# A two-layer attention and gated-MLP kernel on one core: two more score products inside the first layer, score tiles 4 to 7 in other PSUM banks, and the general-weight code moved behind the last batch

## The reference, cut to what matters

```python
xn = layernorm(x)
# attention of the first layer, one head of width 128
k, q, v = xn @ Wk.T, xn @ Wq.T, xn @ Wv.T
ak = k @ Wa.T
alpha = softmax(q @ ak.T)          # 1024 x 1024 scores for each batch
s = alpha @ (v @ Wb.T)
# MLP of the first layer, ternary weights with a scale for each output
h = silu(lin(xn, w1)) * lin(xn, w2)   # the gated units, 512 wide
h = gelu(lin(h, h1)); h = gelu(lin(h, h2))
g = lin(h, w3)
```

## Time and profile before

| | |
|---|---|
| median of three runs | 1051.15 us |
| profiled execution, device time | 1052.17 us |
| its span (first to last instruction) | 1050.3 us |
| TensorE busy | 980.8 us, 93% of the span |
| ScalarE busy | 759.2 us, 72% |
| VectorE busy | 560.3 us, 53% |
| GpSimd busy | 197.7 us, 19% |
| mean granted TensorE clock | 0.988 of full speed |
| one batch, start to start | about 254 us |

### The profile page before, as it was taken

One profiled execution on the slowest core, in us unless ns is written; L12 is line 12 of the kernel. 1 busy time (PEld: TensorE's weight loads), 2 busy tenths in 40 slices (PEclk: granted clock), 3 DMA queues, 4 the chain that ended last, 5 costly groups with the idle time before them and its releaser, 6 DMA issues.

```text
span 1050.3 us, 16258 instructions
## 1 busy us (share of the span) xinstructions
PE 980.8 (93%) x6122; PEld 548.5 (52%) x6122; DVE 560.3 (53%) x1372; ACT 759.2 (72%) x926; POOL 197.7 (19%) x144
## 2 busy tenths in 40 slices
PE   3999899999999989999989989999999998999995
PEld 2788633343478843334358874334436886333431
DVE  6655734635546653554564574455446457346252
ACT  5444699989753479998955358998885436999885
POOL 1100202512300020341130002043122002025023
PEclk9999899999999999999999999999999999999998
DMA  6000032000000013100000002300000000310000
GB/s 239 1 2 1 13 49 50 1 2 1 5 19 2 1 30 49 34 1 2 1 21 2 1 1 46 65 3 1 1 1 21 2 1 13 50 30 1 1 1 23
DMA packets 14428, 20.66 MB, mean 20 GB/s; under 512 B 2848, under 2 KB 11136, under 8 KB 14080
## 3 DMA queue, kind: packets, MB, share of 16 engines
q1 hardware_dynamic: 14336, 19.41, 8.6%
HBM read 7.85 MB, written 2.10 MB: 9 GB/s over the span
## 4 chain that ended last, share of the span: by engine, by line
PE 76%; DVE 8%; ACT 7%; issue 6%; POOL 2%; DMA 0%; DVEq 0%; POOLq 0%; ACTq 0%
PE ps L1097 73%; ACT big L1053 4%; PE ps L1501 1%; DVE st L277 1%; DVE wk L543 1%; POOL st L867 1%; DVE xn L449 1%; DVE wk L733 1%; ACT xn L1025 1%; ACT qz L1001 1%; DVE wk L474 1%; DVE flags L417 1%; PE ps L1117 1%; DVE qk_max L558 0%; PE ps L1494 0%
## 5 line engine op out<-in xcount | busy, mean ns | idle before, releaser
L1053 ACT ACTIVATE big<-ps 128x1024 f32<-128x1024 f32 x512 | 493.8, 1034 | 50.8 <-PE ps L1097 48.7
L1097 PE MATMUL ps<-big,vaug 128*32 128x512 f32 x2048 | 272.6, 604 | 3.8 <-DVE wk L733 2.6
L1097 PE MATMUL ps<-hid 32*128 32x512 f32 x1024 | 130.6, 493 | 3.7 <-ACT big L1053 2.5
L1097 PE MATMUL ps<-hid,fw_sb 128*128 128x512 f32 x416 | 100.7, 396 | 0.0
L969 ACT ACTIVATE wk<-ps,cols_sb 128x512 f32<-128x512 f32 x64 | 40.5, 687 | 78.3 <-PE ps L1097 74.3
L867 POOL TENSOR_TENSOR st<-st 128x4 f32<-128x4 f32 x16 | 16.2, 1011 | 423.3 <-DVE st L532 315.2
L1097 PEld LDWEIGHTS ps<-hid 32*128 32x128 f32 x1024 | 49.1, 181 | 77.2 <-issue 41.6
L1097 PEld LDWEIGHTS ps<-hid,fw_sb 128*128 128x128 f32 x416 | 77.7, 188 | 17.8
L880 POOL TENSOR_TENSOR qz<-qz,wk 128x512 f32<-128x512 f32 x32 | 41.1, 1286 | 232.8 <-DVE wk L703 232.8
L1097 PEld LDWEIGHTS ps<-big,vaug 128*32 128x32 f32 x2048 | 41.0, 108 | 69.8 <-issue 42.2
L721 DVE SCALAR_TENSOR_TENSOR big<-ps,sm,big 128x128 f32<-128x128 f32 x128 | 44.2, 345 | 46.9 <-PE ps L1097 35.9
(11 more groups left out here) (210 smaller groups left out, 1618.5 us busy)
## 6 DMA issues: line engine op xcount, KB each, us to landing
hid<-spl SPq DMA_DIRECT2D x288, 32.0 KB
xnext<-in_x SPq DMA_DIRECT2D x4, 512.0 KB, 3.9
out<-qz SPq DMA_DIRECT2D x8, 256.0 KB, 2.3
big<-in_fw SPq DMA_DIRECT2D x1, 1877.0 KB, 8.9
wk<-in_lw SPq DMA_DIRECT2D x1, 1476.0 KB, 13.9
big<-in_fw SPq DMA_DIRECT2D x1, 939.0 KB, 10.7
cst_sb<-in_cst SPq DMA_DIRECT2D x1, 440.0 KB, 4.4
xn<-in_aw SPq DMA_DIRECT2D x1, 320.0 KB, 5.0
```

The source lines that it names most:

```text
L1053: up(ms_exp, a.activation(prob[:, at:at + 2 * CH].rearrange("p (h n) -> p h n", n=CH), ps[:, bank:bank + 2, :], ACT.Exp, scale=HDM ** -0.5))
L1097: return t_.matmul(out_, lhsT, rhs, start=start, stop=stop, **kw)
```

## The change

Four edits, all in TensorE's program but for one bank table that ScalarE's exponentials read too.

- `SC_BANKS` becomes a table of 16: tiles 0 to 3 and 8 to 15 stay in banks 2, 3, 6, 7, tiles 4 to 7 go to banks 0, 1, 4, 5, those of the gated units 2 and 3. Tile 4 then waits for the gate of unit 2, tile 6 for that of unit 3 (`gated`), tiles 8 to 11 for the exponentials of tiles 0 to 3, tiles 12 to 15 for those of tiles 8 to 11.
- The products of tile 3 are made ahead of `l1_unit(0, 2)`, those of tile 2 behind it, after a wait for `neg_ok` (bank 6 holds the transposed maxima until then). The loop then adds only the maxima to the first four tiles.
- Both `t_.If` are replaced by branches whose exact target stands right behind them.
- The general code of all batches stands once each behind the last batch, and jumps back.

```diff
-MAX_BANKS, SC_BANKS = (2, 6), (2, 3, 6, 7)
+MAX_BANKS, SC_BANKS = (2, 6), (2, 3, 6, 7, 0, 1, 4, 5, 2, 3, 6, 7, 2, 3, 6, 7)
@@ scalar
-                                            ps[:, SC_BANKS[n_ % 4], :], ACT.Exp))
+                                            ps[:, SC_BANKS[n_], :], ACT.Exp))
@@ tensor
                 def score_products(n_):
                     h, jt = n_ // NT, n_ % NT
                     sl = slice(h * CH, (h + 1) * CH)
-                    split3(ps[:, SC_BANKS[n_ % 4], :], *tok(jt), spl[:, 0, sl], spl[:, 1, sl], True, False)
+                    split3(ps[:, SC_BANKS[n_], :], *tok(jt), spl[:, 0, sl], spl[:, 1, sl], True, False)
...
                     t_.transpose(ps[0:NT, 6, 0:P], mx[:, :], ident).then_inc(maxT.sem, 1)
+                    score_products(3)
                     l1_unit(0, 2, general)
+                    t_.wait_ge(neg_ok.sem, neg_ok.at(b, 1))
+                    score_products(2)
                     l1_unit(0, 3, general)

-                with t_.If(wide > 0):
-                    first_layer(True)
-                with t_.Else():
+                t_.br_lt(wide, 1, on_true="t_exact1_%d" % b, on_false="t_general1_%d" % b)
+                with nc.body("t_exact1_%d" % b, valid_engines=[t_.engine]):
                     first_layer(False)
-
-                t_.wait_ge(neg_ok.sem, neg_ok.at(b, 1))
+                    t_.br("t_scores_%d" % b)
+                attended.close()
+                attended.enter_context(nc.body("t_scores_%d" % b, valid_engines=[t_.engine]))
+
                 t_.wait_ge(negrow_in.sem, negrow_in.at(b, 16))
                 for n_ in range(2 * NT):
+                    if n_ in (4, 6):
+                        t_.wait_ge(gated.sem, gated.at(b, n_ // 2 + 1))
+                    elif 8 <= n_ < 12:
+                        t_.wait_ge(sc_exp.sem, sc_exp.at(b, n_ - 7))
+                    elif n_ >= 12:
+                        t_.wait_ge(sc_exp.sem, sc_exp.at(b, n_ - 3))
                     if n_ >= 4:
-                        t_.wait_ge(sc_exp.sem, sc_exp.at(b, n_ - 3))
-                    if n_ >= 2:
                         score_products(n_)
                     h = n_ // NT
-                    up(sc_mm, mm(ps[:, SC_BANKS[n_ % 4], :], one_row[:, :], shift[:, h * CH:(h + 1) * CH], False, True))
+                    up(sc_mm, mm(ps[:, SC_BANKS[n_], :], one_row[:, :], shift[:, h * CH:(h + 1) * CH], False, True))
...
-                with t_.If(wide > 0):
-                    mlp_rest(True)
-                with t_.Else():
+                t_.br_lt(wide, 1, on_true="t_exact2_%d" % b, on_false="t_general2_%d" % b)
+                with nc.body("t_exact2_%d" % b, valid_engines=[t_.engine]):
                     mlp_rest(False)
+                    t_.br("t_second_%d" % b)
+                attended.close()
+                attended.enter_context(nc.body("t_second_%d" % b, valid_engines=[t_.engine]))
...
             for b in range(B):
+                with nc.body("t_general1_%d" % b, valid_engines=[t_.engine]):
+                    first_layer(True)
+                    t_.br("t_scores_%d" % b)
+                with nc.body("t_general2_%d" % b, valid_engines=[t_.engine]):
+                    mlp_rest(True)
+                    t_.br("t_second_%d" % b)
...
```

More of the change, by code:

```diff
@@ L1561, in _ @@
             for b in range(B):
+                with nc.body("t_general1_%d" % b, valid_engines=[t_.engine]):
[4 more added lines that the diff above has]
+                    t_.br("t_second_%d" % b)
+                for s_ in (wblk_used, pv_mm, l1_mm, h_mm, w3_mm, gnat_mm, maxT, max_mm, xT_mm):
+                    s_.given = s_.per * B - s_.left_out
                 with nc.body("t_maxima_%d" % b, valid_engines=[t_.engine]):
```

## The result

The changed kernel takes **1042.9 us** (median of 20 runs) against 1053.92 us for the kernel before (20 runs, same chip): a ratio of 0.9897, 95% interval 0.9879 to 0.9914, or 10.9 us (9.1 to 12.8). One of the 20 executions (1056.08 us) is more than 1.5% above the quickest and is left out of the ratio. The forecast was 9.8 us off, or 1041.4 us in a range of 1038.5 to 1046.5. The profiled execution took 1038.88 us.

What follows compares the result with a forecast made beforehand. TensorE, busy for 93% of the span, was taken to bound the kernel. Score products 6.4 us plus branch gap 3.4 us make 9.8 us off the median 1051.15, giving 1041.4 us, range 1038.5 to 1046.5.

Steps and rivals of the forecast that it cites:

- The base: Median of the kernel before, 1051.15 us, 1.0 us under its profiled execution; the gain was taken off it.
- The pace of the score loop: TensorE, gated unit 3 to second branch: 56 products at 0.232 us in place of 62; 6.4 us over four batches.
- give or take 0.05: TensorE, second batch: gated unit 3 still starts at 295.54, as its gate allows, within 0.05 us.
- The waits put in: Score loop: tiles 4 and 6 wait for gates, met with 0.06 us to spare; missing both leaves 1.47 us a batch.
- The branch's gap: Idle weight load before each batch's first `attend`, behind the second branch: gone with the exact target adjacent, 3.4 us.
- Rival 1: Second branch keeps its gap whatever follows; gain 6.4 us alone, 1044.8 us; chance 0.17.
- A price of a branch that is the same at any distance: Both branches: the number executed stays the same, so moving the code would be worth nothing, in place of 3.4 us.
- Rival 3: Every taken branch costs TensorE's sequencer a fetch; 16 at 0.97 us make 15.5, giving 1056.9 us; chance 0.07.
- Rival 2: Slow clock met less often, or far jump also delayed later code fetches; gain 9.8 + 2.4, 1039.0 us; chance 0.10.
- one piece of 40.70 us: TensorE alone on the chain of waits from the second branch, second batch; held against later fetch stops.
- The clock as no net effect: Slow clock at the second layer's start may shift either way: no net effect, bound 2.4 us on both sides.

Runs made afterwards that it cites:

- code alone: Kernel before with only the general code moved behind the last batch, score products and banks as before; 1051.27 us, ratio 0.9979.
- old banks: Changed kernel with tiles 4 to 7 put back into the four score banks, with the old waits for exponentials; 1050.07 us, ratio 0.9963.
- scores alone: Changed kernel with the general code back inline between branch and exact code; 1049.55 us, ratio 0.9975.
- with filling: Ten unread products added in TensorE's idle time at the second layer's start: kernel before 1050.85 us, scores alone 1047.86, code alone 1046.63, changed kernel 1044.15.
- far pads: Changed kernel with 192, 256, 384 or 512 never-run products, by batch, between second branch and exact code; the two pad kernels took 1043.05 and 1046.09 us.
- banks alone: Changed kernel with the products of tiles 2 and 3 back in the loop, new bank table and moved code kept; 1047.04 us, ratio 0.9978.

## Why the prediction was right, point by point

- **The base: luck.** The 1041.4 us stood on the median of three executions of the kernel before, 1051.15. Twenty gave 1053.92, so the same 9.8 us off would be 1044.1. The base was 2.8 us too low and the gain 1.1 us too small, which partly cancel. The gain is what the mechanism has to answer for, and it is inside its interval.
- **The pace of the score loop: right, 6.1 us for 6.4.** From unit 3 to the branch 13.07 us in the second batch, where 56 x 0.232 made 12.99. Of the 0.08 over it 0.06 are seen: unit 3's first product is followed after 0.29 us (291.15 to 291.44), not 0.23. It came 0.09 us behind its gate; "give or take 0.05" was nearly all used. Over four batches, against code alone, 58.64 - 52.40 = 6.2, less 0.1 for unit 3's later start.
- **The waits put in: both met,** with more room than the 0.06 us foreseen: 0.16 and 0.19 us from the gate's end to the tile's start, since unit 3 came 0.04 us later behind its gate than forecast and lost 0.06 at its first product. The price of missing the banks, by contrast, was far above anything in the prediction: 1.5 us a batch with the old banks.
- **The branch's gap: right, 3.4 us for 3.4**, by distance and not by the branch: code alone removes it, scores alone keep it, unrun products bring it back, and at the other branch too. Rival 1 is out. The distance rested on two places, 27 and 232 products; the step lies between 128 and 192. A price of a branch that is the same at any distance, which the prediction held against itself, is out as well; the section of the Trainium skill that it names there gives two times and says nothing of distance, and "whatever the distance" was my reading. The Trainium skill (Runtime: NRT & Kernel Launch, Instruction fetch mechanics) says that instructions are fetched ahead in sequence, in blocks of 256, and that a taken branch to a target outside the two blocks at hand waits for its block. That fits the step, the flat price, the packets that fell from 60 to 50, and the packet that ends about 1.5 us ahead of every product behind a stop. The same section gives TensorE room for 2048 instructions; the step at some 256 to 384 doesn't show it. That the stop is shorter at the second branch because products were still queued there fits the windows, but was not tested by itself.
- **Rival 3, a price for every taken branch: out.** No branch of the changed kernel shows a stop: the only idle time of TensorE of 0.3 us or more that its trace puts down to "issue" lies at 25.1 us, ahead of all of them, and the kernel before has it too. In the second batch the piece of 55.88 us takes in the plain branch ahead of the score loop and the conditional one behind it.
- **Rival 2, better luck: partly, and in both its halves.** Less time at half pace gave the profiled execution 3.3 us. And the far jump did leave a fetch behind later. A second stop of 0.86, 0.91 and 2.56 us, 16, 15 and 5 products behind the first, stands in three of the 16 batches of the four traces with a general arm in between (before, scores alone, and both with filling), each time in batch 1. Each starts again 1.38 to 1.57 us behind the end of an instruction packet, as the first stops do. The seven traces with exact code right behind its branches have none in 28 batches, and the far pads have none in four. The prediction excluded it by one piece of 40.70 us; that was one execution of a thing that comes and goes. Gaps vary too: 0.84 to 1.35 us for the same code.
- **The clock as no net effect, 2.4 us to each side: the right mean, a bound too narrow.** One execution differs from another by more: the changed kernel's go from 1038.81 to 1056.08 us. Over all timed runs, with one level for each kernel, the time rises by 0.35 us for each us at half clock (worked out from each run's mean granted clock), and within the changed kernel's 20 runs the two go together (correlation 0.86, or 0.77 without the slowest). At equal clock by this line the differences from before are: changed kernel 10.0 us (give or take 1.0), code alone 4.0, scores alone 6.3, old banks 3.7, banks alone 4.9 (1.2 each). The traces say 9.5, 3.4, 6.6, 3.6 and 4.2.

That line, with 4.0 and 6.3 for 10.0, is the likeliest reason why the parts did not add up as timed. Code alone and scores alone ran at a median granted clock of 0.9825 and 0.982, the kernel before and the changed one at 0.987. The 0.0048 between are 2 x 0.0048 x 1050 = 10 us more at half clock, worth 3.5 us in each. This is a correlation, not a test, and the filled kernels do not obey it: the kernel before with filling ran at a median granted clock of 0.994 against 0.985, by the line 6.6 us less, and was 3.4 us quicker by the medians and 1.9 by the ratio. Two reasons are on record. The 0.35 is a mean over places that cost 0.2 and places that cost 0.6. And the mean granted clock misses the program's start in 10 of the 14 traces, where up to 10.2 us at half clock stand in the other four; that alone moves the mean by more than 0.003. What decides where the half clock falls stays open, and so does whether the two parts drew it by chance or by their timing. The second stop, which the change also takes out, may be what the timed 10.9 has over 9.5, but this is argued; the difference lies within the interval.

## What to carry to other kernels

Look at the engine's idle time behind each runtime branch and count the instructions jumped over: an arm that never runs still cost about 1 us here when the taken target lay some 384 instructions on, and nothing at some 256; moving it behind the last batch cost nothing that the traces show. Work brought forward into an engine's gaps needs buffers that come free early enough; reorder and buffers are one edit, and each alone shows little. Where the clock moves single executions by more than the change, cut the trace at marks that both kernels have and sum only the stretches touched, and don't trust a timed difference of parts below half a per cent without the clock beside it. Check that the granted clock is on record for the whole stretch: the distance between equal products tells the pace where it isn't.

## What the runs showed of the hardware

- Jumping over up to 128 weight load and product pairs costs nothing that the trace shows; 192 to 512 cost TensorE 0.85 to 1.1 us where work was queued ahead, and 2.4 to 3.2 us at the other branch (456).
- A product behind such a stop starts 1.38 to 1.68 us after a packet of 16384 bytes has ended on the instruction queue (27 of 27 stops; 0.2 to 23 us, without order, at 36 jumps to a near target).
- Some of the code that is never run is fetched: 60 instruction packets with the general arm inline, 50 without, and 54, 57 and 58 with unrun pads of 480, 1184 and 1824 pairs in all. The last are four pads of 456 pairs and bring two packets each, so the far end of a pad is not fetched.
- A stop of 3.22 us was followed by a granted clock of 0.54 over 6.5 us; stops of 3.22 and 3.09 us cost 5.9 and 5.4 us in all, nearly as much again in slow products as in idle time.
- A fully busy TensorE can be slowed as well: 0.79 over 20 us with TensorE busy for 20.00 of them. A us at half clock cost 0.5 to 0.6 us there and 0.2 us at the start of the second layer.
